# Layer two of a graph network: one half bank added behind every weighing instead of two behind every second

## The chip, the cores and the metric

The kernel runs on one core of one Trainium2 chip. The metric is the device time of one execution in microseconds (us), and a version of the kernel is judged by the median of its runs. A core has five engines, each with its own list of instructions that it works off in order: TensorE (PE, matrix products; its weight loads are listed apart as PEld), VectorE (DVE), ScalarE (ACT), GpSimd (POOL) and SyncE (SP). They wait for one another by semaphores, which are counters.

## What is computed

A two-layer graph attention network over 6250 nodes and 206250 edges, and behind it a layer of eight experts of which each node takes two. What matters here is the sum over the edges in layer two (256 features wide, one head):

```python
h = x @ W.T + b
score = s_src[src] + s_dst[dst]
e = jnp.exp(-jax.nn.leaky_relu(score, ALPHA))
h_prime = jax.ops.segment_sum(e[:, None] * h[dst], src, num_segments=N)
```

Then come a layer norm, an elu and the residual, and the experts:

```python
for e in range(E):
    h = jax.nn.gelu(tokens @ w1[e] + b1[e], approximate=False)
    y = h @ w2[e] + b2[e]
    out = out + combine[:, e:e + 1] * y
```

## The kernel before

The edges are sorted by source node into tiles of 128 edges, so that each tile belongs to one block of nodes (there are 50 blocks). One tile is a **step**. Layer two has 1664 steps (`STEPS`), in 416 groups of four (`GROUP`, number `g`, place in the group `j`); it is built by `aggregate_out`. What each engine does for a step:

- POOL gathers the 128 rows of the target nodes by an indirect DMA (L1355). It may be nine groups ahead: for step s of group g it waits until the product of the step 36 earlier has been counted in `summed`.
- VectorE makes the score of a group (L1384 `add_target`, L1389 `make_leaky`), ScalarE its exponential, the weight (L1462).
- VectorE **weighs**: `weigh(g, j)` (L1394) writes `out_hot`, a 128x128 matrix that holds an edge's weight in the column of its source node, and counts it in `ready`.
- TensorE multiplies `out_hot` by the gathered rows (L1502). An f32 product is two matrix instructions, so layer two has 3328 of them. The 128x256 result fills half a bank of the accumulator memory; three banks (`BANKS`) of two halves (`HALVES`) are used in turn. Two steps that share a bank are a **run**. Each product is counted in `summed`.
- VectorE **adds** each half to the sums of its block in `late_sums` (L1407) and counts it in `taken`. The block's number comes from a register; the 16 numbers of four groups are read by one TENSOR_LOAD (L1324) ahead of the add of every 16th step.

Two waits tie the adds to TensorE. The add of an even step s waits until both halves of its bank are written (`summed` at least s+2), since VectorE and TensorE may not touch one bank at once. And the product of an even step q waits until the bank is free again, which is to say until the add of step q-5 is done:

```python
if step % HALVES == 0 and run >= BANKS:
    pe.wait_ge(s["taken"], base["taken"] + (run - BANKS + 1) * HALVES)
pe.wait_ge(s["ready"], base["ready"] + step + 1)
```

The order of VectorE is written out by hand, group by group. Between the weighings stand `add_target` and `make_leaky` for the group two ahead, `make_turn` (L1371) for the group ten ahead, and the adds. `extra.upto(d)` puts in the work of the other part of the program, the norm and the experts of blocks whose sums are complete (function `experts`; L1822 to L1914 its norm and routing, L1926 and L1931 the sums over experts, L1979 the hidden layer on ScalarE, L2038 and L2055 the experts' products). Each piece has a due step d: on VectorE it stands behind the weighing of step d, on TensorE behind the product of step d. On TensorE a step's product is thus followed by one product of the experts (two matrix instructions) in most steps, and every 16 steps by 16 small products of scores (L1487), behind the product of the step that is 8 modulo 16.

The norm of a block begins at due steps that are at least 12 (`LATE_OUT`) behind the block's last step.

Of the kernel before, what the change touches and what calls it, by code (L numbers as in the profile page):

```python
# [23 lines left out]
ALU = mybir.AluOpType  # L24
# [5 lines left out]
FEAT = 256  # L30
# [22 lines left out]
GROUP = 4  # L53
HALVES = 2
MOST_TILES = (EDGES + P * BLOCKS) // P
LANE_GROUPS = 2
STEPS = -(-MOST_TILES // (GROUP * LANE_GROUPS)) * GROUP * LANE_GROUPS
COLS = -(-STEPS // P) * P
GROUPS = STEPS // GROUP
# [982 lines left out]

AHEAD = 2
LATE = 4
ADDED_LATE = 3
LATE_OUT = LATE + 2 * GROUP


# [245 lines left out]
def aggregate_out(nc, sems, k, s, gathered, lanes_in, table, s_src, node_of, local_of, step_info, lane_rows, sums_of, beside, loads):  # L1294

    with ExitStack() as ctx:
        st = Stage(nc, ctx, sems, "out")
        RING, HOTS, TURNS, BANKS = OUT_RING, 6, 10, 3
        BATCH, LEAD = 4, 6
# [12 lines left out]
        banks = st.ps("banks", [P, BANKS, HALVES, FEAT])  # L1312
        ps_s = st.ps("ps_s", [P, 512])
        base = EACH_TURN
# [6 lines left out]
        def block_ids(engine, first_group):  # L1321

            first, count = first_group * GROUP, min(BATCH, GROUPS - first_group) * GROUP
            _, found = nc.values_load_multi_w_load_instructions(  # L1324
                step_info[96:97, first:first + count], engines=(engine,), min_val=0, max_val=BLOCKS - 1,
                skip_runtime_bounds_check_because="the sort writes them within bounds")
            return [nc.s_assert_within(v, 0, BLOCKS - 1, skip_runtime_bounds_check_because="a block") for v in found]
# [32 lines left out]
        def _(dve):  # L1360
            seq = Chain(dve, s["split"], base["split"])
            extra = Beside(*(work() for work in works["vector"]))
            places = {}

            def make_turn(g):
                n, part = g // LANE_GROUPS, g % LANE_GROUPS
                dve.wait_ge(lanes_in[n % LANE_RING], lanes_base + 16 * (n // LANE_RING + 1))
                if g >= TURNS:

                    dve.wait_ge(s["scored"], base["scored"] + (g - TURNS) // BATCH + 1)  # L1370
                nc.vector.tensor_scalar(hot_t[:, g % TURNS, :],  # L1371
                                        lanes[:, n % LANE_RING, part * GROUP * P:(part + 1) * GROUP * P],
                                        k["iota_p"][:, :], None, ALU.is_equal).then_inc(s["turn_made"], 1)

            def reduce_pieces(batch):
                dve.wait_ge(s["scored"], base["scored"] + batch + 1)
                nc.vector.tensor_reduce(picked[:, batch % 2, :],
                                        ps_s[:, 0:BATCH * GROUP * PIECES].rearrange("p (j c) -> p j c", c=PIECES),
                                        AX.X, ALU.add).then_inc(s["reduced"], 1)

            def add_target(g):
                dve.wait_ge(gathered[g % RING], gathered_base[g % RING] + (g // RING + 1) * 16 * GROUP)
                dve.wait_ge(s["reduced"], base["reduced"] + g // BATCH + 1)
                nc.vector.tensor_tensor(score[:, g % 3, :], picked[:, g // BATCH % 2, g % BATCH * GROUP:(g % BATCH + 1) * GROUP],  # L1384
                                        rows[:, g % RING, :, FEAT], ALU.add).then_inc(s["added"], 1)

            def make_leaky(g):
                dve.wait_ge(s["added"], base["added"] + g + 1)
                nc.vector.scalar_tensor_tensor(score[:, g % 3, :], score[:, g % 3, :], SLOPE, score[:, g % 3, :], ALU.mult, ALU.max)\  # L1389
                    .then_inc(s["leaky"], 1)  # L1390

            def weigh(g, j):
                step = g * GROUP + j
                nc.vector.tensor_scalar(hot[:, g % HOTS, j, :], k["iota"][:, :], local_of[:, step:step + 1],  # L1394
                                        weight[:, g % 3, j:j + 1], ALU.is_equal, ALU.mult).then_inc(s["ready"], 1)

            def add_bank(run):
                for step in range(run * HALVES, (run + 1) * HALVES):
                    if step % (BATCH * GROUP) == 0:
                        places["now"] = block_ids(mybir.EngineType.DVE, step // GROUP)  # L1400
                    place = places["now"][step % (BATCH * GROUP)]
                    if step % HALVES == 0:
                        dve.wait_ge(s["summed"], base["summed"] + (run + 1) * HALVES)
                    if step:
                        dve.wait_ge(s["taken"], base["taken"] + step)
                    here = sums_of[:, bass.ds(place * FEAT, FEAT)]
                    nc.vector.tensor_tensor(here, banks[:, run % BANKS, step % HALVES, :], here, ALU.add).then_inc(s["taken"], 1)  # L1407

            seq.mark(nc.vector.tensor_copy(pieces[:, :, 0], s_src[:, :]))
            seq.wait()  # L1410
# [13 lines left out]
                make_leaky(g)  # L1424
            dve.wait_ge(s["zeroed"], base["zeroed"] + 1)

            for g in range(GROUPS + 2):
                if g < GROUPS:
                    dve.wait_ge(s["is_weight"], base["is_weight"] + g + 1)
                    if g >= HOTS:  # L1430

                        dve.wait_ge(s["summed"], base["summed"] + (g - HOTS + 1) * GROUP)
                    weigh(g, 0)
                if (g + AHEAD + 1) % BATCH == 0 and g + AHEAD + 1 < GROUPS:
                    reduce_pieces((g + AHEAD + 1) // BATCH)
                extra.upto(g * GROUP)
                if g < GROUPS:
                    weigh(g, 1)
                if g + AHEAD < GROUPS:
                    add_target(g + AHEAD)  # L1440
                if ADDED_LATE <= g * HALVES < STEPS // HALVES + ADDED_LATE:
                    add_bank(g * HALVES - ADDED_LATE)
                extra.upto(g * GROUP + 1)
                if g < GROUPS:
                    weigh(g, 2)
                if g + AHEAD < GROUPS:
                    make_leaky(g + AHEAD)
                if g + TURN_AHEAD < GROUPS:
                    make_turn(g + TURN_AHEAD)
                extra.upto(g * GROUP + 2)  # L1450
                if g < GROUPS:
                    weigh(g, 3)
                if ADDED_LATE <= g * HALVES + 1 < STEPS // HALVES + ADDED_LATE:
                    add_bank(g * HALVES + 1 - ADDED_LATE)
                extra.upto(g * GROUP + 3)
            extra.upto(None)

# [663 lines left out]
```

## Time and profile before

| | |
|---|---|
| median of 3 runs | 6315.34 us (6313.79 to 6316.71) |
| the profiled execution | 6255.36 us, its span on the core 6253.6 us |
| layer two in the span | about 3750 to 6190 us |
| PE busy over the span | 81% |
| VectorE busy | 73% |
| POOL busy | 63% |
| mean granted clock of TensorE | 0.900 |

The span is the time from the core's first instruction to its last. A busy time is the sum of an engine's instructions; ends of matrix instructions are modelled. The granted clock is the share of full speed that TensorE was given.

### The profile page before, as it was taken

The page shows a single profiled execution, that of the slowest core. Times are in us where ns is not written, and L with a number is a line of the kernel's source. Part 1 is how long each engine was busy: PE and PEld are TensorE (multiplying, and loading weights), DVE is VectorE, ACT ScalarE, POOL GpSimd, SP SyncE. Part 2 cuts the span into 40 slices and gives each one's busy share as a digit, 9 for nine tenths or more (in the row PEclk, how much of TensorE's full clock was granted, in tenths as well). Part 3 has the DMA queues.
Part 4 walks back from the last instruction along what each step waited for, and adds up shares of the span by engine and source line. Part 5 has one row for each costly group of instructions (what it writes and reads, how often), then busy time and mean ns, then how long its engine had stood idle before and what let it go on. Part 6 is the DMA issues. An engine that isn't in the chain of part 4 may idle for free. (4 is left out here: it accounts for less than half of the span.)

```text
span 6253.6 us, 91913 instructions
## 1 busy us (share of the span) xinstructions
PE 5059.3 (81%) x20985; PEld 2892.5 (46%) x20985; DVE 4552.9 (73%) x15618; ACT 2609.7 (42%) x6620; POOL 3941.8 (63%) x4400
## 2 busy tenths in 40 slices
PE   7878888688888888888888856787888888887888
PEld 4533333333333333333333324666666666666666
DVE  6699999676676777677767755777777777777775
ACT  2278888254444555554554530222222222222223
POOL 2379998466666666666666646666666666666662
PEclk8999999899999999899999977888988888899889
DMA  2200000576677776767777754444444444444441
GB/s 73 64 6 1 1 1 1 150 201 197 199 200 199 207 202 200 200 197 201 200 202 202 201 158 115 119 116 120 119 119 120 117 120 120 118 120 117 119 119 43
DMA packets 323700, 826.45 MB, mean 132 GB/s; under 512 B 73309, under 2 KB 103311, under 8 KB 323187
## 3 DMA queue, kind: packets, MB, share of 16 engines
q0 software_dynamic: 212992, 664.75, 38.4%
q1 hardware_dynamic: 107907, 155.02, 8.5%
q8 instruction: 206, 3.38, 0.2%
q14 instruction: 307, 2.51, 0.1%
q10 hardware_dynamic: 2288, 0.79, 0.1%
HBM read 793.97 MB, written 26.33 MB: 131 GB/s over the span
## 5 line engine op out<-in xcount | busy, mean ns | idle before, releaser
L1106 POOL DMA_INDIRECT heads_rows<-table,shared_node_of x1664 | 1575.4, 947 | 1000.5 <-issue 402.9
L1355 POOL DMA_INDIRECT out_rows<-table,shared_node_of x1664 | 1589.3, 955 | 901.9 <-issue 460.5
L1286 PE MATMUL heads_banks<-heads_rows,heads_hot 128*128 128x512 f32 x3328 | 1894.9, 688 | 160.9 <-DVE heads_rows L1162 101.7
L1229 ACT ACTIVATE sums<-heads_banks x1664 | 970.7, 600 | 1260.6 <-PE heads_banks L1286 841.4
L1502 PE MATMUL out_banks<-out_rows,out_hot 128*128 128x256 f32 x3328 | 1150.1, 438 | 339.6 <-DVE late_sums L1407 242.6
L1162 DVE TENSOR_TENSOR heads_rows<-heads_rows,heads_ps_k 128x512 f32<-128x512 f32 x1664 | 1126.0, 677 | 1.4
L1407 DVE TENSOR_TENSOR late_sums<-out_banks,late_sums 128x256 f32 x1664 | 700.1, 421 | 525.5 <-PE out_banks L1502 197.3
L1502 PEld LDWEIGHTS out_banks<-out_rows,out_hot 128*128 128x128 f32 x3328 | 693.2, 218 | 567.8 <-DVE late_sums L1407 333.4
L1286 PEld LDWEIGHTS heads_banks<-heads_rows,heads_hot 128*128 128x128 f32 x3328 | 542.3, 205 | 503.2 <-issue 474.4
L571 POOL TENSOR_SCALAR sort_plain_lane<-sort_lanes_h,sort_place 125x128 f16<-125x128 f16 x990 | 685.9, 704 | 74.0 <-ACT sort_by_lane L864 42.2
L1462 ACT ACTIVATE out_weight<-out_score 128x4 f32<-128x4 f32 x416 | 85.2, 205 | 1325.3 <-DVE out_score L1389 716.7
L2038 PE MATMUL moe_ps_y<-late_w,moe_hidden 128*125 128x256 f32 x1600 | 544.1, 429 | 87.0 <-DVE moe_result L1931 42.9
L974 PE MATMUL sort_ps_a<-sort_by_tile,sort_by_lane 125*128 125x367 f16 x1650 | 532.1, 326 | 101.1 <-DVE sort_by_tile L742 47.2
L1394 DVE TENSOR_SCALAR out_hot<-const_iota,shared_local_of,out_weight 128x128 f32<-128x128 f32 x1664 | 574.2, 360 | 5.4 <-DVE moe_pick L1904 4.4
L1145 DVE TENSOR_REDUCE heads_score<-heads_ps_s 128x32 f32<-128x96 f32 x416 | 106.0, 255 | 643.1 <-remote 430.5
L974 PE MATMUL sort_ps_b<-sort_by_tile,sort_by_lane 125*128 125x367 f16 x1650 | 524.8, 320 | 0.0
L2055 PE MATMUL moe_ps_h<-moe_tokens_t,late_w 128*128 128x250 f32 x1600 | 506.2, 409 | 0.9 <-ACT moe_hidden L1979 0.5
L742 DVE TENSOR_SCALAR sort_by_tile<-sort_count_all_h,sort_place 125x367 f16<-125x367 f16 x1650 | 481.5, 340 | 4.4 <-PE sort_ps_b L974 4.4
L1283 PEld LDWEIGHTS heads_banks<-heads_zeros 128*128 128x128 bf16 x1664 | 168.0, 101 | 656.1 <-issue 649.0
L1283 PE MATMUL heads_banks<-heads_zeros 128*128 128x2 bf16 x1664 | 284.6, 171 | 208.7 <-issue 112.2
L863 ACT ACTIVATE sort_by_lane<-sort_plain_lane,sort_low 125x128 f16<-125x128 f16 x990 | 391.9, 396 | 93.8 <-PE sort_ps_b L974 89.9
L2038 PEld LDWEIGHTS moe_ps_y<-late_w,moe_hidden 128*125 128x125 f32 x1600 | 327.1, 214 | 167.1 <-issue 108.2
(340 smaller groups left out, 6354.2 us busy)
## 6 DMA issues: line engine op xcount, KB each, us to landing
heads_lanes<-lane_rows SPq DMA_DIRECT2D x208, 256.0 KB
out_lanes<-lane_rows SPq DMA_DIRECT2D x208, 256.0 KB
heads_rows<-table,shared_node_of POOLq DMA_INDIRECT x1664
out_rows<-table,shared_node_of POOLq DMA_INDIRECT x1664
table<-proj_rows SPq DMA_DIRECT2D x50, 227.5 KB
table<-mid_rows SPq DMA_DIRECT2D x50, 113.8 KB
sort_member<-in_x SPq DMA_DIRECT2D x5, 1120.0 KB
moe_x_raw<-in_x SPq DMA_DIRECT2D x50, 112.0 KB
```

What stands on the lines that cost most here:

```text
L571: nc.gpsimd.tensor_scalar(plain_lane[:, made % LANES_AHEAD, :], lanes_h[:, :], lane[:, n:n + 1], None, ALU.is_equal)\
L974: ins = nc.tensor.matmul(ps[:, part % 2, 0:PART_TILES], by_lane[:, slot, number, :], by_tile[:, slot, :], start=False, stop=False)
L1106: nc.gpsimd.indirect_dma_start(out=rows[:, g % RING, j, :], out_offset=None, in_=table[:, :], in_offset=bass.IndirectOffsetOnAxis(ap=node_ ...
L1162: nc.vector.tensor_tensor(by_head, by_head, column(near[:, g % 2, j, :], width // heads), ALU.mult)\
L1229: nc.scalar.activation(sums_of[:, bass.ds(place * width, width)], banks[:, bass.ds(bank, width)], ACT.Copy)\
L1286: nc.tensor.matmul(banks[:, bass.ds(info[j], width)], hot[:, g % HOTS, j, :], rows[:, g % RING, j, 0:width], start=False, stop=True, skip_ ...
L1355: nc.gpsimd.indirect_dma_start(out=rows[:, g % RING, j, :], out_offset=None, in_=table[:, :], in_offset=bass.IndirectOffsetOnAxis(ap=node_ ...
L1394: nc.vector.tensor_scalar(hot[:, g % HOTS, j, :], k["iota"][:, :], local_of[:, step:step + 1], weight[:, g % 3, j:j + 1], ALU.is_equal, AL ...
L1407: nc.vector.tensor_tensor(here, banks[:, run % BANKS, step % HALVES, :], here, ALU.add).then_inc(s["taken"], 1)
L1502: nc.tensor.matmul(banks[:, run % BANKS, step % HALVES, :], hot[:, g % HOTS, j, :], rows[:, g % RING, j, 0:FEAT], start=True, stop=True).t ...
L2038: ins = pe.matmul(sums_ps[:, h, :], hidden[:, number % 4, unit, h * NB:(h + 1) * NB], w2_sb[:, unit, e, :], start=unit == 0, stop=unit == ...
L2055: ins = pe.matmul(hidden_ps[:, number % 2, unit, :], w1_sb[:, q, e, unit * P:(unit + 1) * P], tokens_t[:, pair % 2, q, :], start=q == 0, s ...
```

## The change

A pair of adds stood behind the weighings of j=1 and j=3, seven and six steps behind. Now one add stands behind each weighing, for the half of four steps back. The waits of the adds and of TensorE are the same as before.

```diff
-ADDED_LATE = 3
+ADDED_LATE = 4
...
-            def add_bank(run):
-                for step in range(run * HALVES, (run + 1) * HALVES):
-                    if step % (BATCH * GROUP) == 0:
-                        places["now"] = block_ids(mybir.EngineType.DVE, step // GROUP)
-                    place = places["now"][step % (BATCH * GROUP)]
-                    if step % HALVES == 0:
-                        dve.wait_ge(s["summed"], base["summed"] + (run + 1) * HALVES)
-                    if step:
-                        dve.wait_ge(s["taken"], base["taken"] + step)
-                    here = sums_of[:, bass.ds(place * FEAT, FEAT)]
-                    nc.vector.tensor_tensor(here, banks[:, run % BANKS, step % HALVES, :], here, ALU.add).then_inc(s["taken"], 1)
+            def add_half(step):
+                if not 0 <= step < STEPS:
+                    return
+                run = step // HALVES
+                if step % (BATCH * GROUP) == 0:
+                    places["now"] = block_ids(mybir.EngineType.DVE, step // GROUP)
+                place = places["now"][step % (BATCH * GROUP)]
+                if step % HALVES == 0:
+                    dve.wait_ge(s["summed"], base["summed"] + (run + 1) * HALVES)
+                if step:
+                    dve.wait_ge(s["taken"], base["taken"] + step)
+                here = sums_of[:, bass.ds(place * FEAT, FEAT)]
+                nc.vector.tensor_tensor(here, banks[:, run % BANKS, step % HALVES, :], here, ALU.add).then_inc(s["taken"], 1)
...
-            for g in range(GROUPS + 2):
+            for g in range(GROUPS + ADDED_LATE // GROUP):
...
                     weigh(g, 0)
+                add_half(g * GROUP - ADDED_LATE)
...
                 if g < GROUPS:
                     weigh(g, 1)
+                add_half(g * GROUP + 1 - ADDED_LATE)
                 if g + AHEAD < GROUPS:
                     add_target(g + AHEAD)
-                if ADDED_LATE <= g * HALVES < STEPS // HALVES + ADDED_LATE:
-                    add_bank(g * HALVES - ADDED_LATE)
                 extra.upto(g * GROUP + 1)
                 if g < GROUPS:
                     weigh(g, 2)
+                add_half(g * GROUP + 2 - ADDED_LATE)
...
                 if g < GROUPS:
                     weigh(g, 3)
-                if ADDED_LATE <= g * HALVES + 1 < STEPS // HALVES + ADDED_LATE:
-                    add_bank(g * HALVES + 1 - ADDED_LATE)
+                add_half(g * GROUP + 3 - ADDED_LATE)
                 extra.upto(g * GROUP + 3)
```

VectorE, one group in the middle of layer two (steps 208 to 211), before. The ISA row is the register instruction that carries the add's waits:

```order
L1394 TENSOR_SCALAR out_hot<-const_iota,shared_local_of,out_weight 128x128 [waits shared_agg_summed,shared_agg_is_weight]
L1394 TENSOR_SCALAR out_hot<-const_iota,shared_local_of,out_weight 128x128
L1384 TENSOR_TENSOR out_score<-out_picked,out_rows 128x4 [waits shared_agg_reduced,shared_gathered0]
L1407 ISA [waits shared_agg_taken,shared_agg_summed]
L1407 TENSOR_TENSOR late_sums<-out_banks,late_sums 128x256
L1407 ISA [waits shared_agg_taken]
L1407 TENSOR_TENSOR late_sums<-out_banks,late_sums 128x256
L1394 TENSOR_SCALAR out_hot<-const_iota,shared_local_of,out_weight 128x128
L1389 SCALAR_TENSOR_TENSOR out_score<-out_score 128x4 [waits shared_agg_added]
L1371 TENSOR_SCALAR out_hot_t<-out_lanes,const_iota_p 128x512 [waits shared_agg_scored,shared_lanes_in1]
L1394 TENSOR_SCALAR out_hot<-const_iota,shared_local_of,out_weight 128x128
L1407 ISA [waits shared_agg_taken,shared_agg_summed]
```

The same group after the change (line numbers behind the function have grown by two):

```order
L1394 TENSOR_SCALAR out_hot<-const_iota,shared_local_of,out_weight 128x128 [waits shared_agg_summed,shared_agg_is_weight]
L1409 ISA [waits shared_agg_taken,shared_agg_summed]
L1409 TENSOR_TENSOR late_sums<-out_banks,late_sums 128x256
L1394 TENSOR_SCALAR out_hot<-const_iota,shared_local_of,out_weight 128x128
L1409 ISA [waits shared_agg_taken]
L1409 TENSOR_TENSOR late_sums<-out_banks,late_sums 128x256
L1384 TENSOR_TENSOR out_score<-out_picked,out_rows 128x4 [waits shared_agg_reduced,shared_gathered0]
L1394 TENSOR_SCALAR out_hot<-const_iota,shared_local_of,out_weight 128x128
L1409 ISA [waits shared_agg_taken,shared_agg_summed]
L1409 TENSOR_TENSOR late_sums<-out_banks,late_sums 128x256
L1389 SCALAR_TENSOR_TENSOR out_score<-out_score 128x4 [waits shared_agg_added]
L1371 TENSOR_SCALAR out_hot_t<-out_lanes,const_iota_p 128x512 [waits shared_agg_scored,shared_lanes_in1]
```

The pair of steps 202 and 203 stood behind the weighing of 209 and the pair 204, 205 behind that of 211; now 204 stands behind 208, 205 behind 209, 206 behind 210, 207 behind 211.

VectorE where the block numbers are read, ahead of the add of step 448, before (the first row is the weighing of step 454):

```order
L1394 TENSOR_SCALAR out_hot<-const_iota,shared_local_of,out_weight 128x128
L1389 SCALAR_TENSOR_TENSOR out_score<-out_score 128x4 [waits shared_agg_added]
L1371 TENSOR_SCALAR out_hot_t<-out_lanes,const_iota_p 128x512 [waits shared_agg_scored,shared_lanes_in1]
L1394 TENSOR_SCALAR out_hot<-const_iota,shared_local_of,out_weight 128x128
L1324 TENSOR_LOAD shared_step_info
L1407 ISA [waits shared_agg_taken,shared_agg_summed]
L1407 TENSOR_TENSOR late_sums<-out_banks,late_sums 128x256
```

and after (the first row is the weighing of step 451):

```order
L1394 TENSOR_SCALAR out_hot<-const_iota,shared_local_of,out_weight 128x128
L1409 ISA [waits shared_agg_taken]
L1409 TENSOR_TENSOR late_sums<-out_banks,late_sums 128x256
L1394 TENSOR_SCALAR out_hot<-const_iota,shared_local_of,out_weight 128x128 [waits shared_agg_summed,shared_agg_is_weight]
L1324 TENSOR_LOAD shared_step_info
L1409 ISA [waits shared_agg_taken,shared_agg_summed]
L1409 TENSOR_TENSOR late_sums<-out_banks,late_sums 128x256
```

The read has moved from behind the weighing of step 455 to behind that of 452. The lists of the other engines are unchanged in order.

## Rows read from the trace of the kernel before

**Rows 1.** The page: span and busy times of the engines.

```profile
span 6253.6 us, 91913 instructions
...
PE 5059.3 (81%) x20985; PEld 2892.5 (46%) x20985; DVE 4552.9 (73%) x15618; ACT 2609.7 (42%) x6620; POOL 3941.8 (63%) x4400
```

**Rows 2.** Windows of layer two: stretch, length, busy by engine, PEclk, DMA, GB/s.

```profile
3800.00:4200.00 400.00, 306.56 (x1255) 232.48 (x1256) 273.46 (x1036) 77.60 (x191) 260.15 (x273) 0.80 0.43 117
4200.00:4600.00 400.00, 325.25 (x1415) 249.84 (x1413) 285.58 (x1091) 94.58 (x215) 258.82 (x273) 0.89 0.44 119
...
5400.00:5800.00 400.00, 323.26 (x1403) 248.28 (x1402) 287.83 (x1088) 97.39 (x221) 258.30 (x272) 0.88 0.44 119
...
sum 2380.00, PE 1924.79 PEld 1481.24 DVE 1695.36 ACT 558.47 POOL 1526.06; mean PE 320.80 PEld 246.87 DVE 282.56 ACT 93.08 POOL 254.34
```

**Rows 3.** Chain that ended last, 3800 to 6190 us, shares by line.

```profile
by line: PE out_banks L1502 23.0%; issue 12.9%; PE moe_ps_y L2038 10.2%; DVE late_sums L1407 9.7%; PE moe_ps_h L2055 8.0%; another core or an unknown queue 7.3%; DVE out_hot L1394 6.4%; PE out_ps_s L1487 6.2%; DVE moe_result L1931 2.0%; DVE
```

**Rows 4.** Waits in layer two: who for whom, us, times, longest.

```profile
POOL out_rows L1355 <- PE out_banks L1502: 290.3, 236, 3.1
PE out_banks L1502 <- DVE late_sums L1407: 242.6, 153, 9.2
DVE late_sums L1407 <- PE out_banks L1502: 197.3, 120, 4.1
...
DVE late_sums L1407 <- remote: 162.6, 57, 8.9
```

**Rows 5.** VectorE by line in layer two: busy, mean ns, idle before.

```profile
L1407 DVE TENSOR_TENSOR late_sums<-out_banks,late_sums 128x256 f32 x1664 | 700.1, 421 | 525.5 <-PE out_banks L1502 197.3 <-remote 162.6 <-issue 38.0
L1394 DVE TENSOR_SCALAR out_hot<-const_iota,shared_local_of,out_weight 128x128 f32<-128x128 f32 x1656 | 571.7, 360 | 5.3 <-DVE moe_pick L1904 4.4
```

**Rows 6.** VectorE's timeline around one wait of an add: start, length, instruction.

```profile
4348.52 0.98 DVE L1407 TENSOR_TENSOR late_sums<-out_banks,late_sums 128x256 f32 x2
4349.42 0.59 DVE L1394 TENSOR_SCALAR out_hot<-const_iota,shared_local_of,out_weight 128x128 f32<-128x128 f32 x2
4349.93 0.16 DVE L1384 TENSOR_TENSOR out_score<-out_picked,out_rows 128x4 f32<-128x4 f32 x1
4350.01 0.98 DVE L1407 TENSOR_TENSOR late_sums<-out_banks,late_sums 128x256 f32 x2
4350.91 0.42 DVE L1836 BATCH_NORM_STATS2 moe_stats<-late_sums 125x6 f32<-125x256 f32 x1
4351.36 0.18 DVE L1838 BATCH_NORM_AGGREGATE moe_spread<-moe_stats 125x2 f32<-125x6 f32 x1
4351.46 0.51 DVE L1394 TENSOR_SCALAR out_hot<-const_iota,shared_local_of,out_weight 128x128 f32<-128x128 f32 x1
4351.69 0.28 DVE L1389 SCALAR_TENSOR_TENSOR out_score<-out_score 128x4 f32<-128x4 f32 x1
4351.76 0.34 DVE L1371 TENSOR_SCALAR out_hot_t<-out_lanes,const_iota_p 128x512 bf16<-128x512 bf16 x1
4352.02 0.34 DVE L1394 TENSOR_SCALAR out_hot<-const_iota,shared_local_of,out_weight 128x128 f32<-128x128 f32 x1
4356.31 0.99 DVE L1407 TENSOR_TENSOR late_sums<-out_banks,late_sums 128x256 f32 x2 [3.94 <-PE out_banks L1502]
```

**Rows 7.** TensorE's timeline of the same stretch.

```profile
4351.67 0.59 PE L1502 MATMUL out_banks<-out_rows,out_hot 128*128 128x256 f32 x2
...
4352.54 0.59 PE L1502 MATMUL out_banks<-out_rows,out_hot 128*128 128x256 f32 x2
...
4353.39 0.59 PE L1502 MATMUL out_banks<-out_rows,out_hot 128*128 128x256 f32 x2
...
4354.24 0.59 PE L1502 MATMUL out_banks<-out_rows,out_hot 128*128 128x256 f32 x2
...
4355.10 0.59 PE L1502 MATMUL out_banks<-out_rows,out_hot 128*128 128x256 f32 x2
4355.53 0.58 PE L2055 MATMUL moe_ps_h<-moe_tokens_t,late_w 128*128 128x250 f32 x2
4357.35 0.70 PE L1502 MATMUL out_banks<-out_rows,out_hot 128*128 128x256 f32 x2 [1.24 <-DVE late_sums L1407]
```

**Rows 8.** Granted clock in two neighbouring stretches, columns as in rows 2.

```profile
4418.80:4428.80 10.00, 8.98 (x31) 5.98 (x32) 7.00 (x24) 0.91 (x4) 6.32 (x8) 0.66 0.46 123
4428.80:4438.50 9.70, 9.70 (x47) 8.52 (x47) 8.63 (x34) 4.63 (x8) 6.24 (x8) 1.00 0.46 123
```

**Rows 9.** All reads of block numbers on VectorE: min/median/max ns.

```profile
L1324 DVEq TENSOR_LOAD <-shared_step_info x104: 1095/1099/1348, 3757.6 to 6173.6; - x104
```

## The prediction

> **What bounds the kernel now.** The page comes first [rows 1]: no engine is full. TensorE is busy 81% of the span, VectorE 73%. The change touches layer two alone, so the next view is its windows [rows 2]. From one to the next they hardly differ: in a full window of 400 us TensorE is busy 325 us and VectorE 286 to 288 us. Over the 2380 us of all six, TensorE is busy 1925 us (81%), VectorE 1695 us (71%) and GpSimd 1526 us (64%). A layer of 1664 steps in some 2430 us takes 1.46 us a step, of which VectorE works 1.04 us. Two engines that each have a fifth or more of their time free, and still set the pace, must be waiting for each other, so the chain and the waits are read next.
>
> In the chain [rows 3] the time goes back and forth: TensorE's lines have 23.0 + 10.2 + 8.0 + 6.2 = 47% of it, VectorE's adds 9.7% and its weighings 6.4%, and 20% is "issue" or unknown. The waits [rows 4] say at which place the two meet. TensorE waited 242.6 us in 153 waits for an add (its bank was not free). VectorE's adds waited 197.3 us in 120 waits for a product, and 162.6 us in 57 waits for something that the trace doesn't name. Both directions stop at the same pair of instructions, and this is the pair that the change moves. By line [rows 5] the adds are VectorE's largest item (700.1 us) and have nearly all the idle time (525.5 us); the weighings have none.
>
> One such wait in detail, with steps counted from the layer's start [rows 6, 7]. VectorE weighs steps 412 and 413 at 4349.42, adds steps 406 and 407 at 4350.01, weighs 414 and 415, and is then idle 3.94 us ahead of the add of step 408. That add needs the product of step 409, which TensorE's rows show at 4351.67, ended at 4352.26. The add begins at 4356.31, and meanwhile TensorE did steps 410 to 413 and one product of the experts, up to 4356.11. Then TensorE was idle 1.24 us until the adds had freed a bank. So a count can reach VectorE much later than the row of its product ends, and here it came when TensorE's stream stopped. I don't know why; the trace doesn't show it. What matters is what VectorE had got done before it stopped, since that is what feeds TensorE afterwards.
>
> **The change part by part.** Nothing is computed more or less: 1664 adds of 0.421 us [rows 5] stay.
>
> *The wait within a pair goes.* Two adds in a row take 0.98 us [rows 6], and the second waits until the first is counted. Two weighings in a row wait for nothing and take 0.59 us at 0.34 us each, so they overlap by 0.09 us. Two adds without the wait would be 2 x 0.42 - 0.09 = 0.76 us, which is 0.22 us less a pair. For 832 pairs that is 183 us of VectorE's time. Of this only what lies on the path counts. The chain has 9.7% of 2390 us = 232 us of adds, a third of their 700 us [rows 3, 5], so I take a third of 183: **61 us gained**, with bounds 0 and 183.
>
> The Trainium skill speaks against this gain (VectorE: DVE Perf Modes, section "The DRAIN you can't avoid"): an instruction starts only when the pipe behind the one ahead is empty, and a semaphore between two costs nothing extra. The two rows above, 0.98 us against 0.59 us, don't agree with it: here the pair with a wait takes longer than its two lengths together and the pair without one less. By the rule the 61 us would be nothing.
>
> *TensorE is let go sooner.* The product of an even step q needed the pair that stood behind the weighing of q+1. It now needs the add of q-5, which stands ahead of the weighing of q, so the weighing alone decides. After a stop like the one above, TensorE restarted after two adds (1.24 us with what lies around them); now after one add of 0.42 and one weighing of 0.34 us, 0.76 us. That is 0.45 us sooner.
>
> *The adds need TensorE sooner.* This is the price. The add of an even step s stood behind the weighing of s+7 and now stands behind that of s+4. In the example VectorE would stop behind the weighing of step 412, not of 415. What it did between is from 4349.76 (4349.42 + 0.34, end of the weighing of 412) to 4352.36 (end of that of 415), 2.60 us, of which one pair of adds, 0.90 us up to the next start, would have been done ahead of 412. The remaining **1.7 us** of work (the weighings of 413 to 415, scores, two instructions of the norm) was done before in the shadow of the wait and is now done behind it. TensorE too had steps up to 413 to do and would now have them only up to 412. If the count comes when TensorE's stream ends, it comes one step sooner, which is 0.86 us (4354.24 to 4355.10) [rows 7]. So a wait costs 1.7 - 0.45 = 1.25 us if its end stays where it is, and 1.25 - 0.86 = 0.4 us if its end moves along. I take the middle, 0.82 us, for all 120 + 57 = 177 waits: **145 us lost**, with bounds 70 and 221. I count the unnamed 57 too, since the adds behind them stood at the same instruction.
>
> *The read of the block numbers* takes 1.10 us, 104 times [rows 9]. It was covered by four instructions in the queue (two weighings, 0.28 and 0.34 us between them) and now has a weighing, an add and a weighing, 0.34 + 0.42 + 0.34 = 1.10 us. I take 0.1 us each: **10 us lost**; with no cover at all it would be 114 us. Nothing is queued behind it but VectorE's own add.
>
> *Work that is hidden anyway.* GpSimd's gathers wait for `summed` (290.3 us in 236 waits) [rows 4] and follow TensorE; they are up to 36 steps ahead, so they end no wait here. The norm begins at least 12 steps behind its block's last step; the last add is now 4 behind instead of up to 7, so it only has more room. The end of the layer has its last adds a few steps sooner, under 2 us.
>
> **Sum:** -61 + 145 + 10 = +94 us. The profiled execution took 6255.36 us, 60 us (0.95%) less than the median of the runs, so 6349 us for it; the runs start from 6315.34 us and give **6409 us**, 1.5% more.
>
> **The rivals.**
>
> *Slower by the window, my forecast (chance 0.42).* The distance over which weighing and adding can drift apart shrinks from seven steps to four, and with stops of 2 to 4 us at 1.46 us a step, four is short. Its own range is 6330 to 6530 us. The upper end takes 221 us of loss and none of the gain (+231, 6546 us).
>
> *Faster: the waits don't grow (chance 0.33).* TensorE, let go at the weighing itself, runs closer behind VectorE, so that the product which an add needs is done sooner by what the add has moved. Then the 145 us fall away and VectorE's saving counts more than a third. For it: 242.6 us of TensorE's idle time has the adds as its end, and that wait is gone. Against it: in rows 6 and 7 VectorE stopped, not for want of TensorE's work but for a late count. The gain would be 61 to 183 us, less 10: in the middle 112 us, 6203 us. It decides from the point where a wait costs less than (61 - 10) / 177 = 0.29 us.
>
> *The two cancel (chance 0.15).* Loss at its lower bound of 70 us against a gain of 61 to 80 us: 6303 to 6328 us.
>
> *Slower, and the clock falls too (chance 0.07).* Two neighbouring stretches got 0.66 and 1.00 of the clock [rows 8], and the layer's first window got 0.80 against 0.89 in the next, with 0.244 us busy for a matrix instruction against 0.230 us [rows 2]. If shorter slack makes such stops everywhere, 6% on TensorE's 1925 us is 116 us, of which its share of the chain, 47%, is 55 us: 94 + 55 = +149, 6464 us. The Trainium skill (TensorE: Matmul & The Clock Gate, Part 1) says that the array runs at 1.2 GHz after it has been idle and at 2.4 GHz after it has been kept busy; the two stretches agree with two such levels.
>
> *The pair's wait costs nothing (chance 0.03).* If the longer pair is a matter of the bank it reads and stays when the adds are apart, the sum is +155 us, 6470 us. This is what the section on the DRAIN cited above would make of the gain.
>
> **How the numbers follow.** A difference under about 0.2% (13 us) can't be told from none here. Slower: 0.42 + 0.07 + 0.03 = 0.52, less 0.02 of the first that ends within 0.2%, is 0.50. Within: 0.15 + 0.02 = 0.17. Faster: 0.33. The range leaves out a tenth on each side: below 6190 us the faster rival would need over two thirds of its 183 us, above 6530 us the bounds of the loss are used up.
>
> **What would show it.** If right: VectorE's idle time ahead of the adds grows from 525.5 us; TensorE's wait for `late_sums` is gone, and a wait for `out_hot` of more than 242.6 us stands in its place; no two adds in a row, and adds that start 0.1 us before their neighbour ends. The layer's windows show VectorE busy under 286 us in 400. If wrong: VectorE's idle time ahead of the adds shrinks or stays, with steps below 1.46 us. What would make it wrong most easily is the count that comes late: if what delays it is the full banks themselves, it goes with them, and the 145 us with it.

## The result, and the profile after

The changed kernel takes 6341.29 us (median of 11 runs, 6320.89 to 6356.98), the kernel before 6316.71 us beside it (11 runs, 6312.0 to 6336.2). The ratio is 1.0043, 95% interval 1.0032 to 1.0055: slower by 0.43%, some 25 to 27 us. The prediction had 6409 us, +94 us. The direction held and the size was over three times too large.

One thing about the rows ahead of the prediction has to be known first. They are from an execution of 6255.36 us, which is 57 us under the lowest of the runs of before that were timed beside the changed kernel. On one of the chips that were used later, the kernel before takes 6228.92 to 6266.92 us, so the first profile may be from such a chip; this isn't on record. The kernel before was profiled once more and took 6302.38 us, of which layer two had 26 us more than in the first profile. Against this second profile the comparison is fairer, and it is called *the second profile of before* below. The profiled execution after took 6350.2 us.

The page after, to be read beside [rows 1]:

```profile
span 6348.5 us, 91913 instructions
...
PE 5048.3 (80%) x20985; PEld 2866.5 (45%) x20985; DVE 4500.7 (71%) x15618; ACT 2610.9 (41%) x6620; POOL 3958.0 (62%) x4400
```

The second profile of before has the same number of instructions in a span of 6300.7 us, and these busy times:

```profile
PE 5088.1 (81%) x20985; PEld 2900.9 (46%) x20985; DVE 4559.5 (72%) x15618; ACT 2608.7 (41%) x6620; POOL 3941.0 (63%) x4400
```

The count of instructions is the same and VectorE works 59 us less (4559.5 to 4500.7), yet the span is longer. Where the layer begins and ends is read from two views by tile and line. TensorE's products, second profile of before ("to" stands between the first start and the last):

```profile
L1502 PE MATMUL out_banks<-out_rows,out_hot x3328: 376/379/796, 3770.2 to 6236.1; 128*128 128x256 f32 x196
```

and after:

```profile
L1504 PE MATMUL out_banks<-out_rows,out_hot x3328: 376/379/797, 3790.2 to 6287.3; 128*128 128x256 f32 x196
```

From first to last product layer two grew from 2465.9 to 2497.1 us, by 31 us; the other 17 us between the two spans lie ahead of the layer, which begins 20.0 us later, in a part that the change doesn't touch. A window of layer two in the second profile of before:

```profile
4200.00:4600.00 400.00, 327.37 (x1404) 251.86 (x1403) 284.31 (x1075) 94.69 (x217) 256.35 (x270) 0.88 0.44 118
```

and after:

```profile
4200.00:4600.00 400.00, 315.21 (x1395) 242.45 (x1394) 271.18 (x1062) 94.17 (x214) 257.03 (x268) 0.88 0.44 117
```

VectorE fell from 284 us in 400 to 271 us, as forecast, and TensorE from 327 to 315 us. The granted clock is the same in this window, and over the 2380 us from 3800 to 6180 it is 0.85 in both profiles, so the clock is out of it. VectorE's adds by line, second profile of before:

```profile
L1407 DVE TENSOR_TENSOR late_sums<-out_banks,late_sums 128x256 f32 x1664 | 701.4, 422 | 551.6 <-remote 212.7 <-PE out_banks L1502 178.4 <-issue 29.9
```

and after:

```profile
L1409 DVE TENSOR_TENSOR late_sums<-out_banks,late_sums 128x256 f32 x1664 | 698.9, 420 | 751.6 <-PE out_banks L1504 431.5 <-remote 253.7 <-issue 60.3
```

The idle time ahead of the adds grew by 200 us ([rows 5] have 525.5 us for the first profile). It also changed its kind. The named causes of before add up to 421.0 us (212.7 + 178.4 + 29.9), and the waits named next add 18.7 us; the remaining 112 us are 0.13 us for each of 832 pairs, the gap inside a pair. After, the causes add up to 745.5 us and 6 us remain. So the gap inside the pairs is gone, and the stops, as waits that have a name or "remote" or "issue" for their end are called from here on, have grown by 306 us. TensorE's waits for VectorE after, beside [rows 4]:

```profile
PE out_banks L1504 <- DVE out_hot L1394: 187.1, 111, 6.2
...
PE moe_ps_y L2040 <- DVE moe_result L1933: 134.4, 66, 6.5
```

and in the second profile of before:

```profile
PE out_banks L1502 <- DVE late_sums L1407: 267.4, 153, 7.5
...
PE moe_ps_y L2038 <- DVE moe_result L1931: 28.4, 32, 3.5
```

TensorE's wait for an add is gone and a smaller one for a weighing stands in its place. A second one has grown that the prediction didn't name: the experts' products wait for VectorE's sums over experts, 134.4 us after against 28.4 us before. Those sums stand in VectorE's queue behind the add that stops. VectorE's timeline at one stop of the changed kernel:

```profile
4499.90 0.34 DVE L1394 TENSOR_SCALAR out_hot<-const_iota,shared_local_of,out_weight 128x128 f32<-128x128 f32 x1
4502.46 0.43 DVE L1409 TENSOR_TENSOR late_sums<-out_banks,late_sums 128x256 f32 x1 [2.22 <-remote]
4502.80 0.34 DVE L1394 TENSOR_SCALAR out_hot<-const_iota,shared_local_of,out_weight 128x128 f32<-128x128 f32 x1
4503.05 0.42 DVE L1409 TENSOR_TENSOR late_sums<-out_banks,late_sums 128x256 f32 x1
```

Each of these instructions starts 0.09 us before its neighbour ends (the weighing at 4502.80 against 4502.46 + 0.43, the add at 4503.05 against 4502.80 + 0.34). The stop of 2.22 us stands ahead of the add of an even step, 472, with one weighing done since the add ahead of it. Its count came late, as in [rows 6, 7]: the product of step 473 had ended at 4498.55, 3.9 us before the add began.

### The profile page after: what moved, and what is told of

It reads as the page before. It is cut to its first block and busy times, and to the rows that moved or that the text cites. A ratio compares the mean times of both kernels' runs of the same rounds, so it can differ in the third digit from the quotient of the medians.

```text
span 6348.5 us, 91913 instructions
## 1 busy us (share of the span) xinstructions
PE 5048.3 (80%) x20985; PEld 2866.5 (45%) x20985; DVE 4500.7 (71%) x15618; ACT 2610.9 (41%) x6620; POOL 3958.0 (62%) x4400
## 5 line engine op out<-in xcount | busy, mean ns | idle before, releaser
L1504 PE MATMUL out_banks<-out_rows,out_hot 128*128 128x256 f32 x3328 | 1151.7, 439 | 243.9 <-DVE out_hot L1394 187.1
L1409 DVE TENSOR_TENSOR late_sums<-out_banks,late_sums 128x256 f32 x1664 | 698.9, 420 | 751.6 <-PE out_banks L1504 431.5
L2040 PE MATMUL moe_ps_y<-late_w,moe_hidden 128*125 128x256 f32 x1600 | 575.6, 450 | 246.6 <-DVE moe_result L1933 136.6
L1394 DVE TENSOR_SCALAR out_hot<-const_iota,shared_local_of,out_weight 128x128 f32<-128x128 f32 x1664 | 598.6, 360 | 8.6 <-remote 7.5
L2057 PE MATMUL moe_ps_h<-moe_tokens_t,late_w 128*128 128x250 f32 x1600 | 483.9, 394 | 3.0 <-issue 2.4
```

The costliest lines, as they stand in the source:

```text
L1504: nc.tensor.matmul(banks[:, run % BANKS, step % HALVES, :], hot[:, g % HOTS, j, :], rows[:, g % RING, j, 0:FEAT], start=True, stop=True).t ...
L2040: ins = pe.matmul(sums_ps[:, h, :], hidden[:, number % 4, unit, h * NB:(h + 1) * NB], w2_sb[:, unit, e, :], start=unit == 0, stop=unit == ...
L2057: ins = pe.matmul(hidden_ps[:, number % 2, unit, :], w1_sb[:, q, e, unit * P:(unit + 1) * P], tokens_t[:, pair % 2, q, :], start=q == 0, s ...
```

## The experiments

Kernels that ran on the same chip share the runs of the kernel before. Three chips gave 6302, 6310 and 6314 us for it (the first, second and third chip), a fourth 6248 us, and a fifth 5442 us, 14% less. Each ratio is to before on the same chip, with its 95% interval.

**How far back.** Only the distance is changed; in the versions for other distances than four the end of the loop over the groups is rounded up, so that the last adds are still made.

```diff
-ADDED_LATE = 4
+ADDED_LATE = 6          # 5, 3 in the others
...
-            for g in range(GROUPS + ADDED_LATE // GROUP):
+            for g in range(GROUPS - (-ADDED_LATE // GROUP)):
```

> One add behind every weighing, but for the half of six steps back. This is the pair of before taken apart, its first half one weighing sooner, so the wait inside the pair goes and the slack stays nearly as it was. Window theory (slack of four steps is too short, the pair's wait is worth about 60 us): 6250 us, faster than before by 50 to 70. Rival (the spacing of adds gives nothing since VectorE isn't the bound; the distance is all): 6310 to 6320, as before. Rival (single adds themselves cost, by the register read with less cover or otherwise): 6340, as the changed kernel.

> One add behind every weighing, for the half of five steps back. Window theory: between the kernels with four and six, 6290 us. If distance means nothing: as the changed kernel, 6340 us.

And the kernel before with its pairs nearer, behind the weighing of s+5 for s+7:

```diff
-ADDED_LATE = 3
+ADDED_LATE = 2
```

> Pairs as before, but each behind the weighing five steps after its first half instead of seven. The wait within the pair stays, the slack is as short as in the changed kernel. Window theory: the loss without the gain, 6316 + 25 + 60 = 6400 us, clearly slower than the changed kernel. Rival (distance means nothing, TensorE is let go two weighings sooner): 6300 to 6316 us. Between the two, 6340 us, if the pair's wait is worth nothing.

> The kernel before, unchanged, for a second profile: its first profiled execution was 57 us below the lowest of its eleven timed runs, while the changed kernel's profile lies within its runs. Expected 6310 to 6340 us, with the layer-two part 20 to 40 us longer than the 2441 us of the first profile (then the true growth of layer two by the change is about 20 to 35 us, not 57) or the difference all ahead of layer two, in the untouched part (then it is 57).

These four ran on the first chip (before 6301.96 us). Six back: 6298.05 us, 0.9991 (0.9979 to 1.0003). Five back: 6302.87 us, 1.0003 (0.9991 to 1.0014). Pairs nearer: 6313.31 us, 1.0009 (0.9998 to 1.002). Before again: 6302.38 us, under the 6310 to 6340 us that were expected, with layer two 26 us longer than in the first profile, as expected. Single adds with one step less slack than before should have won 50 to 70 us and won 4 us by the medians, and not clearly. Two steps less slack with pairs should have cost about 85 us; it cost 11 us by the medians and may have cost nothing. Both terms were too large. In five back the even adds stand where they stand in the nearer pairs, but single: 10 us less by the medians. That would be the price of the pair's wait on the path, but the two intervals overlap.

A second chip (before 6309.95 us) had the changed kernel and six back side by side.

> The changed kernel once more. The two sets of runs so far were on two chips: on one the kernel before takes 6302 us and counts reach VectorE and GpSimd late, on the other it takes 5442 us, no such late counts show, and GpSimd's gathers, one every 1.25 us, set the pace of layer two. If late counts are what makes the slack of four too short: +0.4% again on a chip of the first kind, and within 0.1% of the kernel before on one of the second kind. If the slack costs by itself, without late counts: +0.4% on both.

> Six steps back once more. On a chip with late counts -0.1% again; on one without, equal to the kernel before and to the changed one within 0.1%, since GpSimd sets the pace.

The changed kernel 6335.86 us, 1.0036 (1.0021 to 1.0051); six back 6301.2 us, 0.9984 (0.9973 to 0.9995). Six back is thus faster than both kernels, by 0.16% and 0.5%, and its interval leaves out 1 here, which it didn't quite on the first chip. Last, three back, on two chips.

> One add behind every weighing, for the half of three steps back. The kernels with six, five and four stand at -0.1%, 0.0% and +0.4% against the kernel before. Window theory (the slack between weighing and product runs out): the loss grows faster than in a line, 6400 to 6460 us, +1.5% to +2.5%. Rival (the +0.4% of four is a matter of that one place in the order, such as the block numbers read behind the weighing of a group's first step): the kernel with three is no worse than that with four, 6325 to 6345 us.

> The half of three steps back behind every weighing, beside the changed kernel. On a chip where counts come late (before near 6310 us): theory 'slack too short' expects more than the changed kernel's +0.4%, by the +1.9% of the other chip at least +1.5%, 6400 us or more. Rival 'the loss at four back is not one of slack' expects about the same as the changed kernel, under +0.7%, below 6355 us. On a chip where they don't (before near 5442 us): +1.9% again, 5550 us, by both.

> The changed kernel, for the comparison on the same chip. Where counts come late: +0.4% as before, 6325 to 6345 us. Where they don't (before near 5442 us), which has not been timed with the real block numbers: theory 'four back costs only where counts come late' expects within 0.1% of before, 5437 to 5448 us; rival 'four back costs on any chip' expects +0.3 to 0.5%, 5459 us or more.

Three back: 5551.65 us on the fifth chip, 1.0192 (1.0173 to 1.0211), and 6364.55 us on the fourth, 1.0185 (1.0163 to 1.0207). The changed kernel on the fourth: 6267.69 us, 1.0035 (1.0023 to 1.0047). Where a time of its own was expected, it had a chip near 6310 us in view; the ratios came out as expected (at least 1.5% more for three back, 0.4% for four). The four comparisons of the changed kernel with before, the first and those on the second, third and fourth chip, agree within 0.1%. With the runs in one row: six back -0.1%, five back 0.0%, four back +0.4%, three back +1.9%. The loss is a steep function of the slack.

Which stops grow with it can be counted from the traces. For the add of an even step, the trace shows when the product that it needs had ended. A stop of over 0.5 us is called *late* if the add begins over 1 us after that end, and any stop is called *real* if the add begins within 0.3 us of it, so that VectorE did wait for TensorE's work. Number of stops ahead of even adds and their sum in us, counted by this rule:

| profile | late | real | first to last product |
|---|---|---|---|
| before, first chip | 144, 329 | 4, 4 | 2465.9 us |
| six back, first chip | 252, 584 | 17, 14 | 2458.0 us |
| five back, first chip | 236, 573 | 37, 35 | 2466.7 us |
| pairs nearer, first chip | 196, 414 | 42, 39 | 2478.6 us |
| six back, second chip | 247, 581 | 22, 18 | 2461.3 us |
| four back, second chip | 199, 542 | 142, 161 | 2497.3 us |
| four back, fourth chip | 200, 512 | 131, 156 | 2466.0 us |
| three back, fourth chip | 166, 418 | 249, 324 | 2556.1 us |

The late stops don't grow as the slack shrinks from six to three; the real ones do, and on each chip the layer's length with them. And the late ones grow by 255 us from before to six back, with a layer that is 8 us shorter: the time that VectorE saved was spent in longer stops.

**Letting TensorE go sooner.** The changed kernel, but the product of an even step also waits for the next weighing. Before, it waited in effect for that weighing and for the pair behind it.

```diff
-pe.wait_ge(s["ready"], base["ready"] + step + 1)
+pe.wait_ge(s["ready"], base["ready"] + step + (2 if step % HALVES == 0 else 1))
```

> The changed kernel, but the product of an even step waits for the weighing of the odd step behind it too, so TensorE is let go about where the kernel before let it go. Nothing else moves. If letting TensorE go sooner is worth what I took (0.45 us in each of some 177 stops, and nothing else), +80 us on the changed kernel: +1.7% against before. If it is worth little, since VectorE stops for a product anyhow, the same as the changed kernel: +0.4 to +0.6%.

> The changed kernel with the product of an even step waiting for the next weighing too. On a chip with late counts: +0.4% as the changed kernel if letting TensorE go sooner is worth nothing, up to +1.7% if it is worth what I took.

> The changed kernel, for the reference on this chip: +0.4% where counts come late, within 0.1% where they don't.

On the fifth chip 5447.72 us, 1.0011 (0.9997 to 1.0024), without the changed kernel itself beside it. On the third, 6341.84 us, 1.0048 (1.003 to 1.0066), beside the changed kernel's 6341.25 us, 1.0041 (1.0024 to 1.0057). Undoing the release costs 0.6 us by the medians. It is worth nothing that can be measured, and the 0.45 us that I credited for each of 177 stops (80 us in all) are not found in the time.

This run also says something of the way by which VectorE's stops reach TensorE. TensorE's waits on the third chip, changed kernel:

```profile
PE out_banks L1504 <- DVE out_hot L1394: 172.1, 105, 6.2
PE moe_ps_y L2040 <- DVE moe_result L1933: 133.9, 67, 6.2
```

and with the release undone:

```profile
PE out_banks L1504 <- DVE out_hot L1394: 271.5, 147, 5.8
PE moe_ps_y L2040 <- DVE moe_result L1933: 58.3, 49, 4.7
```

The wait of the experts' products fell to less than half, and a longer wait for a weighing took its place, at the same time of execution (6341.25 and 6341.84 us). At which of its instructions TensorE waits for VectorE thus made no difference here.

**The read of the block numbers.** Both kernels with block numbers that are known when the program is built, so that the 104 reads on VectorE fall away. They come from an even division of the steps among the blocks, so that sums near a border land in the neighbouring block.

```diff
-                if step % (BATCH * GROUP) == 0:
-                    places["now"] = block_ids(mybir.EngineType.DVE, step // GROUP)
-                place = places["now"][step % (BATCH * GROUP)]
+                place = step * BLOCKS // STEPS
```

> The changed kernel with VectorE's adds going to blocks fixed in the program (step times 50 over 1664) instead of numbers read at run time: the 104 reads of 1.10 us and the register instruction of each add go, and sums may land in another block than the edges' own. If the read with less cover is what the change costs: this kernel and the same edit on the kernel before are within 0.1% of each other. If the window costs it: this one is slower by 20 to 30 us than the other. By itself the edit should give 10 to 60 us in both.

> The kernel before with the same fixed blocks (sums may land in another block than the edges' own). The partner of the run above: 6240 to 6295 us; what counts is the distance between the two.

> The changed kernel with blocks fixed in the program (sums may land in another block than the edges' own), once more. On a chip with late counts: if the read of the block numbers makes the +0.4%, it falls to that of the partner below; if the slack makes it, it stays 20 to 30 us above the partner.

> The partner: the kernel before with fixed blocks (sums may land in another block than the edges' own). Within 0.2% of the kernel before.

The fifth chip: changed 0.9995 (0.9985 to 1.0005), before 0.9998 (0.9988 to 1.0008). By the expectation, two equal times speak for the reads as the cause; but on this chip something else covers the cost of four back (below), so the third chip has to decide. The third chip: changed 6323.34 us, 1.0012 (0.9997 to 1.0026), before 6299.96 us, 0.9979 (0.9963 to 0.9996). On the third chip the distance between the two is 23 us without the reads and was 27 us with them. The reads explain some 4 us of it, and that difference is itself within the intervals. The reads and the register instructions of the adds together cost 14 us in the kernel before and 18 us in the changed one.

The kernel before without the reads shows one thing more. Its adds still stand in pairs, and the second still waits until the first is counted, but no register instruction stands between them. A pair on the third chip:

```profile
4603.46 0.87 DVE L1405 TENSOR_TENSOR late_sums<-out_banks,late_sums 128x256 f32<-128x256 f32 x2
```

It takes 0.87 us where a pair with the register instruction takes 0.98 us [rows 6]; the medians over all 832 pairs are 0.88 and 0.99 us. So half of the 0.22 us that the prediction put down to the wait belong to the register instruction.

On the fifth chip, with the block numbers fixed, four back costs nothing, 0.9 us between the medians. VectorE's adds there, before without the reads:

```profile
L1405 DVE TENSOR_TENSOR late_sums<-out_banks,late_sums 128x256 f32<-128x256 f32 x1664 | 699.7, 421 | 49.7 <-PE out_banks L1500 19.2 <-issue 1.3
```

and changed without the reads:

```profile
L1407 DVE TENSOR_TENSOR late_sums<-out_banks,late_sums 128x256 f32<-128x256 f32 x1664 | 691.9, 416 | 163.0 <-PE out_banks L1502 160.2
```

The idle time ahead of the adds, 551.6 us in the second profile of before, is 49.7 us here, and no stop is unnamed or late. The change lets it grow to 163.0 us as well. All of its 185 stops, 160 us, are real ones, as many us as on the second chip, yet the layer grows by 3 us only. GpSimd's gathers show why. In the kernel before with fixed block numbers one gather begins 1.25 us (median) after the last, which is the layer's pace (2071.6 us for 1664 steps), and none waits for a product longer than 0.3 us (first row); in the kernel with three back some do (second row):

```profile
POOL out_rows L1355 <- PE out_banks L1500: 81.0, 266, 0.3
```

```profile
POOL out_rows L1355 <- PE out_banks L1504: 179.7, 318, 4.9
```

By these rows another engine sets the pace on this chip, and it covers what four back costs. That was not tried alone; three back, with 367 real stops of 418 us, is past what it covers, and the layer takes 2178.1 us. The changed kernel with its own block numbers was not timed on this chip.

**The copies of the lane numbers.** Can the transfers on SP's queue be what delays the counts? In both kernels the copies of `out_lanes`, from the ring's second round on, move an eighth of their rows. The scores of layer two are then not those of the reference.

```diff
-                first, count = n * LANE_GROUPS * GROUP, LANE_GROUPS * GROUP
-                sp.dma_start(lanes[:, n % LANE_RING, :],
+                first, count = n * LANE_GROUPS * GROUP, LANE_GROUPS * GROUP if n < LANE_RING else 1
+                sp.dma_start(lanes[:, n % LANE_RING, 0:count * P],
```

> The changed kernel with the broadcast of lane numbers in layer two (256 KB every eight steps) cut to 32 KB from the third on, so the one-hot rows of most steps are stale and the scores wrong. If the late counts come from this burst of transfers: on a chip of the first kind layer two falls from 1.49 us a step to near 1.25 and the whole by 300 us or more. If not: within 20 us of the changed kernel. On a chip of the second kind nothing in either case.

> The same cut on the kernel before. If the burst makes the counts late and late counts make the slack too short, this kernel and the changed one with the same cut are equal within 0.1%; otherwise the distance of 0.4% stays.

On the second chip: changed 6331.75 us, 1.0036 (1.0022 to 1.005), before 6304.9 us, 0.9999 (0.9987 to 1.0012). Nothing changes, so these copies are not the cause. The two are also the one pair of profiles of before and after from one chip with the reads in: layer two has 2469.9 and 2499.5 us, 30 us more, which agrees with the 31 us of the section on the result, whose two profiles may be from different chips.

## Why the prediction was wrong in its size

*The frame held.* The layer is bound by two engines that wait for one another at the adds; the change moves that place; less slack costs time. VectorE's busy time in a window (271 us, forecast under 286), the end of the pairs, the overlap of 0.1 us, TensorE's wait for `late_sums` gone, and idle time ahead of the adds above 525.5 us (751.6 us) were all as forecast. The wait for `out_hot` was not: 187.1 us, where more than 242.6 us were forecast.

*The pair's wait goes: 61 us forecast.* As VectorE's time it was sized well: 0.22 us x 832 = 183 us, against 59 us less work and 112 us less gap, 171 us. Half of it is the register instruction between the adds and not the wait: without it a pair takes 0.87 us and not 0.98. The 0.87 us are still more than the 0.76 us that two adds without a wait would take. The Trainium skill (VectorE: DVE Perf Modes, section "The DRAIN you can't avoid") says that the semaphore costs nothing extra; the rows of this case don't agree, by 0.11 us a pair. What failed in this term is "a third of it lies on the path". Six back against before is -4 us on one chip and -9 us on another, with one step less slack for the even adds, and five back against the nearer pairs is -10 us, where the intervals overlap. That is 4 to 10 us, 2 to 6% of 171 us. The rest came back as a longer stop at the next add. A share of the chain says how much time went through an instruction, not what comes back when it gets shorter, in a loop where the same engine then waits for the other.

*The adds need TensorE sooner: 145 us forecast.* This is the step that failed. In its place: seven to five steps costs 11 us or less (the nearer pairs), and five to four 21 to 25 us (from 1.0003 to 1.0036 or 1.0043, on other chips). Counted as I did, from before to four back with the small gain of single adds given back, the term is about 25 or 27 us and 4 to 10 us more, 29 to 37 us. I priced every one of 177 stops at 0.82 us of the layer's time, by the example of a stop whose count came late. Such stops don't grow with less slack (581 us at six back, 542 us at four), and they are no measure of length: from before to six back they grew by 255 us and the layer shrank. What grew with the layer are real stops, of which the kernel before has hardly any: 4 us before, 161 us at four back. Of the 306 us by which all stops grew, some 200 us are there at six back already. From six to four, on one chip, VectorE's idle time ahead of the adds grew from 648.3 to 759.9 us and the layer by 36 us.

*The release of TensorE: 0.45 us a stop.* Measured as nothing (0.6 us in all). By the prediction's own numbers it would be 1.24 - 0.76 = 0.48 us, which changes the sum by 5 us.

*The read: 10 us.* Not confirmed; some 4 us, within the intervals.

*The rivals.* "The waits don't grow" is refuted: 440 us of stops ahead of the adds became 745.5 us. "The two cancel" (6303 to 6328 us) is nearer to the 6341 us than my forecast is, but misses it too; both terms are small, and what is left over is a small loss. The clock stayed where it was. That the direction was right owes something to luck: the two large terms were both over three times too large, and their difference kept its sign.

**Where the loss between five and four comes from** is shown as far as the slack of the even add: the reads, the release and the lane copies are excluded, the loss continues steeply to three, and the real stops grow with it. It does not hang on late counts: on the fifth chip, which has none at four back and 14 us of them at three back, the real stops grow just as much, and three back costs 109 us; that four back costs nothing there is, by the rows of the gathers, because GpSimd sets the pace. How the stops become TensorE's time is not resolved to one place. It is tempting to name the sums over experts, which stand in VectorE's queue behind the stopped add and for which the experts' products wait (28.4 us before, 134.4 us after). But that wait has 113.1 us at five back, which costs nothing, and 132.1 us at three back, which costs most, and with the release undone it fell from 133.9 to 58.3 us without a gain.

## What to carry to other kernels

Where two engines exchange halves of a buffer in a loop, the price of the distance between them is not a straight line: measure one step more and one less before pricing it, since here five steps cost nothing clear of noise, 4 cost 0.4% and 3 cost 1.9%. Ask of a stop whether the work that it waits for had just ended: such stops grew with the loss here, and stops for a late count did not. If an operation is split to save the wait between its parts, keep the distance of the earliest part nearly as it was: single adds at six steps back gave the one version with right sums that was faster than before (0.9984, 0.9973 to 0.9995, on the second of two chips). And an idle time that grows is not a loss of that size: 306 us more of stops were 31 us of layer, and six back has some 200 us more of stops in a layer 8 us shorter.

## What the runs showed of the hardware

The same kernel took 6302 to 6314 us on three chips, 6248 us on a fourth and 5442 us on a fifth. On the fifth, VectorE's adds wait for nothing unnamed, and the layer's 1664 steps take 2071.6 us from first to last product (kernel before with fixed block numbers) against 2465.9 us in the second profile of before. On the others VectorE stops ahead of an add whose product had ended well before, as in [rows 6, 7]: in the second profile of before 144 stops with 329 us began over 1 us after the product's end. Of its 74 unnamed waits (212.7 us, the longest 7.4 us) those ahead of even adds all ended 1.6 us or more after the product. What makes a count late on one chip and not on another stays open. It is not the copies of lane numbers and not the reads of block numbers.

Two 128x256 adds of which the second waits until the first is counted take 0.98 us with a register instruction between them and 0.87 us without; two weighings of 0.34 us that don't wait for one another take 0.59 us.
